# Row products of a patch-attention kernel, made once per feature row and kept

## The chip, the cores and the metric

The kernel runs on one core of a Trainium2 chip. The metric is the device time of one launch in microseconds (us), the median of several runs. In what follows TensorE is PE, VectorE is DVE, ScalarE is ACT, GpSimd is POOL, and SyncE (the engine that issues nearly all DMAs here) is SP.

## The reference

The input x has the shape (4, 64, 80, 80). Two identical layers of contextual attention run one after the other, each on 4 images, so there are eight units of work. One layer, cut to what matters:

```python
f = b[:, :, ::2, ::2]                                   # 64 x 40 x 40
w = 3x3 patches of f                                    # L = 1600 positions, 576 values each
wn = w / max(||w||, 1e-4)
yi = einsum('bpd,bld->blp', w, wn) * mm                 # 1600 x 1600 scores
yi = softmax(yi * 10, axis=1) * mm
patches = einsum('blp,bld->bpd', yi, 4x4 patches of b)  # pasted back with overlap
out = overlap_add(patches) / 4
```

The score of two positions is the sum, over the nine taps of a 3x3 window, of the products of 64 channels.

## The kernel before

**Tiles.** The 40 feature rows, padded to a pitch of 41, are laid out in 3 strips of 14 rows. A row tile holds the same row of the 3 strips, which is 3 x 41 = 123 positions (TW). There are 14 row tiles (TILES), worked on in 7 pairs (PAIRS), and 16 with the border. The scores of a unit, G, are a matrix of 14 x 14 blocks of 123 x 123; its columns are worked on in four chunks. S_CHUNKS (line 28) gives the chunks of the scores: 2, 4, 4 and 4 blocks. P_CHUNKS (line 27) gives those of the second part: 4, 4, 4 and 2. A "score pair" j (0 to 27) is one pair of row tiles t, t+1 (t = 2(j mod 7)) in one chunk k = j div 7. The matrix is symmetric before it is scaled, so blocks below the diagonal are not computed again: they are transposed on PE from blocks already in G.

**Three taps by three.** Call P(r, c) the product of feature row tile r with row tile c, summed over the three horizontal taps. The score block of row tile t and column s is P(t, s) + P(t+1, s+1) + P(t+2, s+2). Features are kept as a float16 high and low part, so that P(r, .) takes 5 matmuls (one_row, line 462): three of HL with LH, one of H1 with H1, one of HL with HL.

**A score pair with products (19 of the 28; nine more only transpose, and three of the 19 do both).** On PE even_tile (line 483) first makes the two rows that both tiles share, P(t+1)+P(t+2), as 9 matmuls in PSUM bank 2 (FREE), and then P(t) as 5 matmuls in bank 0. odd_tile (line 498) makes P(t+3) as 5 matmuls in bank 1; in ten pairs one column block can't use the shared rows and takes 14 matmuls of one block (TERMS, line 456 on), so such a pair has 33. ACT's copy_shared (line 656, activation in line 670) brings the shared rows from PSUM to the odd tile's place in G, one block further on (in the last chunk to S); copy_scores (line 672, activation in line 683) brings the transposed blocks and the lone blocks. DVE's score_pair (line 856) adds the shared rows to bank 0 for the even tile (tensor_tensor in line 881), takes the maximum of the scaled result (line 887, which also writes the scaled scores to S), adds and takes the maximum for the odd tile, and negates both maxima (line 892). Each maximum waits for the add in front of it on the same engine. ACT's score_sums (line 685, exp in line 697) then sums the exponentials of S.

**The other half of a slot.** The work is written out by hand in slots (body functions, s = 2 to 29), the same list on every engine, and skewed between units: while unit v's scores are made, unit u = v-1 goes through its second part. In each slot DVE runs, in this order, argument_pair (line 941) for the pair four slots on, add_shifted (line 952) for two slots on, after a shifted copy that SP issued as DMAs (SH<-G, line 326) has landed, sum_pair (line 974) for one slot on, and then score_pair. ACT runs the copies, with softmax_pair (line 708) between those of the even and of the odd tile, and then score_sums of the pair before. PE runs even_tile, two matmuls of paste_tile (line 521, float32, two records each), odd_tile and two more of paste_tile. Slots 16 and 21 hold two score pairs (score_list, line 48), slots 28 and 29 none. The features of the next unit but one are made in slots 5 and 6 on ACT (lines 612 to 624) and DVE (line 819), and laid out by SP in slots 10 to 12 (line 307: HL, H1, HV). SP stores results (line 314) in slots 8, 15, 22 and 29 and loads the next image (line 270) in slot 9. In slots 23, 24, 28 and 29 DVE and ACT work out the logarithms of the softmax sums (lines 906 to 931, 729, 734).

**Lead-in and tail.** Unit 0's scores have no second part beside them, and unit 7's second part has no scores beside it. Seven stretches hold both.

## Time and profile before

| | us |
|---|---|
| median of 3 runs | 1446.03 (1445.3 to 1454.68) |
| the profiled execution, its own time | 1450.82 |
| its span in the profile | 1449.0 |
| granted TensorE clock, mean | 0.986 of full |

The profile gives for each engine the time in which it was busy, the chain of work that ended last, and for each instruction group what ended the idle time before it. PE counts as busy until the modelled end of a matmul; matmuls overlap by about the time that one takes to drain, so the distance between two starts is what a matmul costs, and its own duration is more. The same is true on a smaller scale of DVE and ACT: an instruction that waits for nothing starts about 0.07 us before the one ahead has ended.

### The profile page before, as it was taken

The page shows a single profiled execution, that of the slowest core. Times are in us where ns is not written, and L with a number is a line of the kernel's source. Part 1 is how long each engine was busy: PE and PEld are TensorE (multiplying, and loading weights), DVE is VectorE, ACT ScalarE, POOL GpSimd, SP SyncE. Part 2 cuts the span into 40 slices and gives each one's busy share as a digit, 9 for nine tenths or more (in the row PEclk, how much of TensorE's full clock was granted, in tenths as well). Part 3 has the DMA queues.
Part 4 walks back from the last instruction along what each step waited for, and adds up shares of the span by engine and source line. Part 5 has one row for each costly group of instructions (what it writes and reads, how often), then busy time and mean ns, then how long its engine had stood idle before and what let it go on. Part 6 is the DMA issues. An engine that isn't in the chain of part 4 may idle for free.

```text
span 1449.0 us, 24232 instructions
## 1 busy us (share of the span) xinstructions
PE 1326.1 (92%) x7190; PEld 892.3 (62%) x7190; DVE 1190.6 (82%) x2827; ACT 856.0 (59%) x2233; POOL 46.8 (3%) x62
## 2 busy tenths in 40 slices
PE   4987999999999999999999899999999999998796
PEld 4756755667556765577556676566755676566333
DVE  4668889789887988888797898979988798978883
ACT  2667646666457664576455864567645765558331
POOL 1000000010000100001000010001000010000100
PEclk9997999999999999999999999999999999999999
DMA  5502482135822555135641357313582236313442
GB/s 90 88 1 84 108 172 74 45 112 119 164 63 60 129 111 148 49 85 129 128 121 34 92 127 161 89 45 99 122 169 65 63 105 136 99 36 86 133 137 55
DMA packets 180469, 142.53 MB, mean 98 GB/s; under 512 B 119858, under 2 KB 177266, under 8 KB 180338
## 3 DMA queue, kind: packets, MB, share of 16 engines
q1 hardware_dynamic: 180178, 140.50, 41.1%
q8 instruction: 57, 0.93, 0.3%
q10 hardware_dynamic: 160, 0.49, 0.2%
q14 instruction: 74, 0.61, 0.1%
HBM read 19.76 MB, written 13.11 MB: 23 GB/s over the span
## 4 chain that ended last, share of the span: by engine, by line
DVE 36%; PE 27%; issue 11%; ACT 9%; SPq 9%; DMA 6%; DVEq 1%; POOL 0%; ACTq 0%; POOLq 0%
PE psG L471 11%; PE psO L521 11%; DVE G L941 9%; DVE Z L974 7%; DVE G L881 5%; DVE S L887 5%; DVE G L952 5%; SPq L326 4%; DMA SH<-G 4%; ACT S L697 3%; PE psG L480 3%; ACT G L708 3%; SPq L270 2%; ACT G L683 2%; SPq L314 2%
## 5 line engine op out<-in xcount | busy, mean ns | idle before, releaser
L521 PE MATMUL psO<-Z,B 123*128 123x492 f32 (+2 forms) x1792 | 711.9, 526 | 41.5 <-DVE Z L974 29.6
L521 PEld LDWEIGHTS psO<-Z,B 123*128 123x128 f32 x1792 | 323.2, 193 | 240.2 <-issue 124.6
L471 PE MATMUL psG<-LH,HL 128*123 128x246 f16 (+2 forms) x2616 | 406.7, 285 | 13.6 <-DVE G L881 10.7
L471 PEld LDWEIGHTS psG<-LH,HL 128*123 128x123 f16 x2616 | 276.1, 137 | 136.7 <-issue 64.4
L708 ACT ACTIVATE G<-G,nb 123x492 f32<-123x492 f32 (+1 forms) x448 | 267.9, 642 | 137.4 <-DVE G L941 136.4
L887 DVE CUSTOM_DVE_ANT_0 S<-G,RB 123x492 f32<-123x492 f32 (+1 forms) x448 | 268.9, 606 | 86.7 <-DVE G L881 55.7
L697 ACT ACTIVATE S<-S,nm 123x480 f32<-123x480 f32 (+3 forms) x560 | 306.8, 554 | 1.8 <-DVE nm L892 1.6
L952 DVE TENSOR_TENSOR G<-G,SH 123x492 f32<-123x492 f32 (+1 forms) x448 | 246.9, 589 | 47.9 <-DMA SH<-G 47.8
L941 DVE SCALAR_TENSOR_TENSOR G<-G,RA,psB 123x492 f32<-123x492 f32 (+1 forms) x448 | 269.9, 645 | 0.0
L683 ACT ACTIVATE G<-psG 123x492 f32<-123x492 f32 (+3 forms) x256 | 119.6, 471 | 147.3 <-PE psG L480 69.1
L974 DVE TENSOR_TENSOR Z<-G 123x984 f32<-123x984 f32 (+2 forms) x192 | 196.8, 1025 | 0.0
L471 PE MATMUL psG<-H 128*123 128x123 f16 (+3 forms) x872 | 193.5, 283 | 0.0
L670 ACT ACTIVATE G<-psG 123x246 f32<-123x246 f32 (+1 forms) x136 | 64.1, 471 | 190.5 <-PE psG L471 190.1
L881 DVE TENSOR_TENSOR G<-G,psG 123x492 f32<-123x492 f32 (+2 forms) x272 | 133.8, 492 | 48.9 <-PE psG L471 28.2
L480 PEld LDWEIGHTS psG<-idn,G 123*123 123x123 f32 x672 | 95.6, 191 | 68.7 <-ACT G L683 22.7
L480 PE MATMUL psG<-idn,G 123*123 123x123 f32 x672 | 110.9, 285 | 23.9 <-ACT G L683 15.0
L471 PEld LDWEIGHTS psG<-H 128*123 128x123 f16 x872 | 102.3, 136 | 21.1 <-issue 0.4
L471 PE MATMUL psG<-HL 128*123 128x492 f16 (+2 forms) x392 | 111.5, 284 | 0.0
L697 ACT ACTIVATION_READ_ACCUMULATOR S<-S,nm 123x1 f32 x560 | 107.7, 192 | 0.0
L1082 POOL COPY G<-G 123x246 f32<-123x246 f32 x56 | 42.7, 771 | 1309.5 <-DVE mx L887 1175.7
L717 ACT ACTIVATE OSB<-psO 128x492 f32<-128x492 f32 (+2 forms) x64 | 31.4, 548 | 71.5 <-PE psO L521 71.3
L471 PE MATMUL psG<-HV 128*123 128x246 f16 (+2 forms) x240 | 67.5, 281 | 0.0
(79 smaller groups left out, 577.2 us busy)
## 6 DMA issues: line engine op xcount, KB each, us to landing
SH<-G SPq DMA_DIRECT2D x336, 214.8 KB
SH<-G SPq DMA_DIRECT2D x112, 89.2 KB
SH<-G SPq DMA_DIRECT2D x336, 19.2 KB
XP<-x SPq DMA_DIRECT2D x20, 280.0 KB, 5.5
XP<-mid SPq DMA_DIRECT2D x20, 280.0 KB, 5.3
HL<-LH SPq DMA_DIRECT2D x16, 246.5 KB, 4.3
mid<-OSB SPq DMA_DIRECT2D x48, 80.0 KB, 2.3
out<-OSB SPq DMA_DIRECT2D x48, 80.0 KB, 2.3
```

What stands on the lines that cost most here:

```text
L471: last = pe.matmul(psG[0:TW, bank, b0 * TW:b1 * TW], st[:, v % 2, p:p + TW], mv[:, v % 2, lo:lo + n], start=i == 0, stop=i == len(terms) - 1)
L480: last = pe.transpose(psG[0:TW, par, i * TW:(i + 1) * TW], G[:, c:c + TW], idn[0:TW, 0:TW])
L521: last = pe.matmul(psO[:, b, 0:n], B[:, o:o + 128], Z[:, 2 * (s % 2) + j, 0:n], start=t == 0, stop=t == TILES - 1)
L670: act.activation(to, psG[0:TW, FREE, stored * TW:w * TW], ACT.Copy).then_inc(p_copied, 1)
L683: act.activation(G[:, c:c + n], psG[0:TW, par, 0:n], ACT.Copy).then_inc(part if shared else read, 1)
L697: last = act.activation(y, y, ACT.Exp, bias=nm[:, k * TILES + t:k * TILES + t + 1], accum_out=sg[:, c:c + 1])
L708: act.activation(y, y, ACT.Exp, bias=nb[:, bass.ds(u * TILES + t, 1)]).then_inc(y_made, 1)
L881: dve.tensor_tensor((odd if par else even)[:, b0 * TW:n], rows[:, p0 * TW:p0 * TW + n - b0 * TW], psG[0:TW, par, b0 * TW:n], ALU.add).then ...
L887: dve.tensor_tensor_reduce(S[:, slot + par, 0:n], (odd if par else even)[:, 0:n], RB[:, s0 * TW:s0 * TW + n], 1.0, 0.0, ALU.mult, ALU.max, ...
L941: dve.scalar_tensor_tensor(out=g, in0=g, scalar=RA[:, bass.ds(u * TILES + t, 1)], in1=psB[0:TW, k % 2, 0:n], op0=ALU.mult, op1=ALU.subtrac ...
L952: dve.tensor_tensor(g, g, SH[:, o % SFREE, 0:n], ALU.add).then_inc(y1_made, 1)
L974: dve.tensor_tensor(Z[:, slot:slot + 2, 0:n], g[:, 2 * i:2 * i + 2, c0:c0 + n], g[:, 2 * i - 1:2 * i + 1, c0 - TW:c0 - TW + n], ALU.add).t ...
```

## The change

The kernel makes P(r, .) once for a chunk and keeps it. A score pair makes two rows, "row2" = P(t+2) and "row3" = P(t+3), 5 matmuls each; P(t) and P(t+1) are left from the pair before. At the start of a chunk's products "first" and "second" are made as well. The three PSUM banks are used in turn by a list of fills (FILLS, 67 a unit). ACT copies even rows to their own place in G and odd rows to a new tile ODD (copy_row), and for the chunk to the right it saves the fourth block of a row in KEPT and brings it back as the block in front of the next chunk's row. DVE does three additions (add_rows): two = ODD + row2, even = own + two, odd = two + row3. The odd tile's maximum and the negation of a pair are moved into the next pair's score_pair, between these additions; pairs 22 and 27 do them at once. The transposes of both tiles of pairs 9, 18 and 27 share a bank. HV and its two DMAs are gone. On ACT lse_log of slot 24 stands ahead of the second copy.

Counted over one unit, from the two lists: matmuls of products 515 (204 of one block, 140 of two, 5 of three, 166 of four) become 230 (30 of two, 30 of three, 170 of four); transposes stay 84. ACT's copies 51 become 104 (31 of three blocks, 42 of one, 18 of four, 13 of two; 18 of the single ones read KEPT). DVE's additions 38 become 58: (10 of two, 10 of one, 17 of four, 1 of three) become (20 of two, 11 of three, 26 of four, 1 of one). Maxima stay 56.

```diff
-def pair_blocks(j):
+def pair_of(j):
     k, t = j // PAIRS, 2 * (j % PAIRS)
     s0, w = S_CHUNKS[k]
-    if t < s0:
-        return w, w, w, 0
-    stored = t - s0 if t < s0 + w else 0
-    alone = stored + 1 if k in (0, NK - 1) or stored else 0
-    return w, stored, alone, w - stored
-SHARED = [j for j in range(SLOTS) if pair_blocks(j)[3]]
-EVEN_PARTS = [j for j in SHARED if pair_blocks(j)[1]]
-ODD_PARTS = [j for j in SHARED if pair_blocks(j)[2]]
+    return k, t, s0, s0 + w, s0 + w if t < s0 else t if t < s0 + w else s0
+def has_products(j):
+    k, t, s0, end, a = pair_of(j)
+    return a < end
+def is_start(j):
+    k, t, s0, end, a = pair_of(j)
+    return j == 0 or (k > 0 and t == s0 - 2)
+def shared_from(j):
+    k, t, s0, end, a = pair_of(j)
+    return a - 1 if k == 0 or t > s0 and a > s0 else a
+def fills_of(j):
+    k, t, s0, end, a = pair_of(j)
+    if not has_products(j):
+        return ["even", "odd"] + (["first", "second"] if is_start(j) else [])
+    return (["first", "second"] if is_start(j) else []) + ["row2", "row3"] + (["both"] if a > s0 else [])
+PRODUCTS = [j for j in range(SLOTS) if has_products(j)]
+FILLS = [(j, kind) for j in range(SLOTS) for kind in fills_of(j)]
+COPIED = [(j, kind) for j, kind in FILLS if kind in ("row2", "row3") and pair_of(j)[1] < TILES - 2]
+def row_of(j, kind):
+    k, t, s0, end, a = pair_of(j)
+    base = 0 if j == 0 else s0
+    return {"first": base, "second": base + 1, "row2": t + 2, "row3": t + 3}[kind]
+def takes_kept(j, kind):
+    k, r = j // PAIRS, row_of(j, kind)
+    return k > 0 and (kind in ("first", "second") or r >= 4 * k + 2)
+def keeps(j, kind):
+    k, r = j // PAIRS, row_of(j, kind)
+    return k < NK - 1 and (j, kind) in COPIED and r >= 4 * k + 2
+TAKEN = [(j, kind) for j, kind in FILLS if ((j, kind) in COPIED or kind in ("first", "second")) and takes_kept(j, kind)]
...
-            TERMS = [(HL, LH, dy, dx) for dy in range(3) for dx in range(3)]
-            TERMS += [(H1, H1, dy, 0) for dy in range(3)]
-            TERMS += [(HV, HV, 0, 2), (HL, HL, 2, 2)]
-            SHARED_ROWS = [(HL, LH, dy, dx) for dy in (1, 2) for dx in range(3)]
-            SHARED_ROWS += [(H1, H1, 1, 0), (H1, H1, 2, 0), (HV, HV, 1, 2)]
-            def one_row(dy):
-                return [(HL, LH, dy, dx) for dx in range(3)] + [(H1, H1, dy, 0), (HL, HL, dy, 2)]
...
+            ROW = [(HL, LH, dx) for dx in range(3)] + [(H1, H1, 0), (HL, HL, 2)]
+            def products(v, j, kind):
+                k, t, s0, end, a = pair_of(j)
+                c0, r = 4 * k, row_of(j, kind)
+                b0, b1 = 0, 4
+                if kind in ("first", "second"):
+                    b1 = 2 if kind == "first" else 3
+                elif t == TILES - 2:
+                    b0 = (shared_from(j) if kind == "row2" else a) + 2 - c0
+                n, bank = fill(v, j, kind)
+                if n >= BANKS:
+                    pe.wait_ge(released[bank], n // BANKS)
+                for i, (st, mv, dx) in enumerate(ROW):
+                    lo, p = (c0 + b0) * TW + dx, r * TW + dx
+                    last = pe.matmul(psG[0:TW, bank, b0 * TW:b1 * TW], st[:, v % 2, p:p + TW],
+                                     mv[:, v % 2, lo:lo + (b1 - b0) * TW], start=i == 0, stop=i == len(ROW) - 1)
+                last.then_inc(filled, 1)
+            def transposes(v, j, kind):
+                k, t, s0, end, a = pair_of(j)
+                n, bank = fill(v, j, kind)
+                pe.wait_ge(*done(v, (k - 1) * PAIRS + (s0 + 2) // 2 if t < s0 else j - 1, "row3"))
+                pe.sem_inc(pe_gate, 1)
+                pe.wait_ge(released[bank], n // BANKS)
+                o = 0
+                for tile in {"even": (t,), "odd": (t + 1,), "both": (t, t + 1)}[kind]:
+                    for s in range(s0, min(a, end)):
+                        c = s * GLEN + tile * TW
+                        last = pe.transpose(psG[0:TW, bank, o:o + TW], G[:, c:c + TW], idn[0:TW, 0:TW])
+                        o += TW
+                last.then_inc(filled, 1)
+            def first_half(v, j):
+                if not has_products(j):
+                    transposes(v, j, "even")
+                    return
+                if is_start(j):
+                    products(v, j, "first")
+                    products(v, j, "second")
+                products(v, j, "row2")
...
+            def copy_row(u, v, j, kind):
+                k, r = j // PAIRS, row_of(j, kind)
+                n, bank = fill(v, j, kind)
+                even, start = r % 2 == 0, kind in ("first", "second")
+                if even:
+                    columns_free(u, k, r)
+                    blocks = 3 if keeps(j, kind) else 2
+                    c = r * GLEN + 4 * k * TW
+                    to = G[:, c:c + blocks * TW]
+                    before = G[:, c - TW:c]
+                else:
+                    blocks = 3
+                    slot = 0 if j == 0 and start else (j + 1) % 2
+                    to = ODD[:, slot, TW:4 * TW]
+                    before = ODD[:, slot, 0:TW]
+                    reader = last_products(v, j)
+                    if reader[0] >= 0:
+                        act.wait_ge(*done(*reader, "row2"))
+                        act.sem_inc(act_gate, 1)
+                if takes_kept(j, kind):
+                    act.wait_ge(row_copied, copied(v, (k - 1) * PAIRS + (r - 2) // 2, "row3" if r % 2 else "row2"))
+                    act.activation(before, KEPT[:, r - 2, :], ACT.Copy).then_inc(kept_taken, 1)
+                act.wait_ge(filled, n + 1)
+                last = act.activation(to, psG[0:TW, bank, 0:blocks * TW], ACT.Copy)
+                if keeps(j, kind):
+                    if takes_kept(j, kind):
+                        act.wait_ge(kept_taken, v * len(TAKEN) + TAKEN.index((j, kind)) + 1)
+                    last = act.activation(KEPT[:, r - 2, :], psG[0:TW, bank, 3 * TW:4 * TW], ACT.Copy)
+                if start:
+                    last.then_inc(released[bank], 1)
+                else:
+                    last.then_inc(row_copied, 1)
...
                     if s % PAIRS == 0 and v is not None:
                         score_sums(v, score_list(s - 1)[0] - 1)
                     for n, j in enumerate(pairs):
-                        if pair_blocks(j)[3]:
-                            copy_shared(u, v, j)
-                        copy_scores(u, v, j, 0)
+                        copy_first(u, v, j)
                         if at and n == 0 and s != 24:
                             softmax_pair(at)
-                        copy_scores(u, v, j, 1)
+                        if s == 24:
+                            lse_log(v, False)
+                        copy_second(u, v, j)
                         if s == 23:
                             lse_exp(v, False)
-                        if s == 24:
-                            lse_log(v, False)
                         if j and (s + 1) % PAIRS:
                             score_sums(v, j - 1)
...
-            def score_pair(v, j):
+            def add_rows(u, v, j):
+                k, t, s0, end, a = pair_of(j)
+                qa, c0 = shared_from(j), 4 * k
+                n = (end - qa) * TW
+                slot = 2 * (j % 2) + 1
+                cols = lambda tile, s, e: G[:, tile * GLEN + s * TW:tile * GLEN + e * TW]
+                two = cols(t + 1, qa + 1, end + 1) if k < NK - 1 else S[:, slot, (qa - s0) * TW:(end - s0) * TW]
+                rows = lambda kind, c, e: psG[0:TW, fill(v, j, kind)[1], (c - c0) * TW:(e - c0) * TW]
+                if k == NK - 1:
+                    dve.wait_ge(s_read, v * NB + 2 * j + 2)
+                    dve.sem_inc(dve_gate, 1)
+                elif u is not None:
+                    if k == 0:
+                        dve.wait_ge(wrap_made, u * PAIRS + min(t // 2 + 2, PAIRS))
+                        dve.sem_inc(dve_gate, 1)
+                    dve.wait_ge(z_made, u * SLOTS + k * PAIRS + min(t // 2 + 2, PAIRS) + 1)
+                    dve.sem_inc(dve_gate, 1)
+                if (j, "row2") in COPIED:
+                    dve.wait_ge(row_copied, copied(v, j, "row2"))
+                else:
+                    dve.wait_ge(row_copied, copied(v, j - 1, "row3"))
+                    dve.sem_inc(dve_gate, 1)
+                    dve.wait_ge(filled, fill(v, j, "row2")[0] + 1)
+                o = (qa - c0 + 2) * TW
+                dve.tensor_tensor(two, ODD[:, j % 2, o:o + n], rows("row2", qa + 2, end + 2),
+                                  ALU.add).then_inc(done(v, j, "row2")[0], 1)
+                yield
+                dve.wait_ge(*done(v, j, "row2"))
+                own = cols(t, a, end)
+                dve.tensor_tensor(own, own, two[:, (a - qa) * TW:n], ALU.add).then_inc(even_added, 1)
+                yield
+                dve.wait_ge(even_added, v * len(PRODUCTS) + count(PRODUCTS, j))
+                dve.sem_inc(dve_gate, 1)
+                if (j, "row3") in COPIED:
+                    dve.wait_ge(row_copied, copied(v, j, "row3"))
+                else:
+                    dve.wait_ge(filled, fill(v, j, "row3")[0] + 1)
+                b = a
+                if k == NK - 1 and qa == a:
+                    first = cols(t + 1, a, a + 1)
+                    dve.tensor_tensor(first, first, rows("row3", a + 2, a + 3), ALU.add).then_inc(odd_begun, 1)
+                    b = a + 1
+                odd = cols(t + 1, b, end)
+                with_two = odd if k < NK - 1 else two[:, (b - 1 - qa) * TW:(end - 1 - qa) * TW]
+                dve.tensor_tensor(odd, with_two, rows("row3", b + 2, end + 2),
+                                  ALU.add).then_inc(done(v, j, "row3")[0], 1)
...
+            def score_pair(u, v, j):
+                adds = add_rows(u, v, j) if has_products(j) else iter(())
+                next(adds, None)
+                if j - 1 not in (-1, 22):
+                    maxima(v, j - 1, 1)
+                next(adds, None)
+                if j - 1 not in (-1, 22):
+                    negate(v, j - 1)
+                next(adds, None)
+                maxima(v, j, 0)
+                if j in (22, SLOTS - 1):
+                    maxima(v, j, 1)
+                    negate(v, j)
```

## Rows read from the trace of the kernel before

**Rows 1.** The page, part 1: busy us (share of the span) xinstructions
```profile
PE 1326.1 (92%) x7190; PEld 892.3 (62%) x7190; DVE 1190.6 (82%) x2827; ACT 856.0 (59%) x2233; POOL 46.8 (3%) x62
```

**Rows 2.** Windows, busy (xcount), of one full unit by chunk of the scores
```profile
839.90:875.10 35.20, 34.08 (x260) 25.70 (x259) 31.88 (x77) 23.00 (x58) 1.84 (x2) 1.00 0.51 123
875.10:923.80 48.70, 48.37 (x205) 28.11 (x205) 42.32 (x88) 24.80 (x57) 0.00 (x0) 1.00 0.69 148
923.80:961.00 37.20, 35.21 (x160) 21.19 (x158) 30.65 (x78) 21.57 (x55) 0.00 (x0) 1.00 0.19 52
961.00:997.50 36.50, 33.49 (x207) 26.12 (x208) 29.74 (x80) 29.69 (x90) 0.00 (x0) 1.00 0.31 85
```

**Rows 3.** The chain that ended last, in order of time: start, length, what
```profile
919.63 1.18 DVE Z L974
...
930.95 1.66 PE psO L521 x4
```

**Rows 4.** Timeline of DVE, one slot with a four-block pair (pair 11)
```profile
910.58 1.36 DVE L941 SCALAR_TENSOR_TENSOR G<-G,RA,psB 123x492 f32<-123x492 f32 x2
...
914.11 0.66 DVE L881 TENSOR_TENSOR G<-G,psG 123x492 f32<-123x492 f32 x1
914.96 0.67 DVE L887 CUSTOM_DVE_ANT_0 S<-G,RB 123x492 f32<-123x492 f32 x1 [0.19 <-DVE G L881]
...
915.55 0.67 DVE L881 TENSOR_TENSOR G<-G,psG 123x492 f32<-123x492 f32 x1
...
917.20 0.72 DVE L941 SCALAR_TENSOR_TENSOR G<-G,RA,psB 123x492 f32<-123x492 f32 x1
```

**Rows 5.** Groups by form, DVE's additions of fewer blocks
```profile
L881 DVE TENSOR_TENSOR G<-G,psG 123x246 f32<-123x246 f32 x72 | 29.0, 403 | 10.5 <-PE psG L471 6.4 <-ACT G L670 3.0 <-ACT G L683 1.1
L881 DVE TENSOR_TENSOR G<-G,psG 123x123 f32<-123x123 f32 x72 | 20.1, 279 | 15.6 <-ACT G L683 14.8
L881 DVE TENSOR_TENSOR G<-S,psG 123x369 f32<-123x369 f32 x8 | 4.3, 535 | 0.6 <-ACT G L683 0.5 <-issue 0.2
```

**Rows 6.** Timeline of PE: products of four blocks, and of one
```profile
705.79 1.41 PE L471 MATMUL psG<-LH,HL 128*123 128x492 f16 x6
...
716.78 0.68 PE L471 MATMUL psG<-LH,HL 128*123 128x123 f16 x9
```

**Rows 7.** Timeline of ACT (exps of one pair, next copy); groups of copies
```profile
909.12 0.69 ACT L697 ACTIVATE S<-S,nm 123x480 f32<-123x480 f32 x1
...
910.47 0.57 ACT L670 ACTIVATE G<-psG 123x492 f32<-123x492 f32 x1
...
L683 ACT ACTIVATE G<-psG 123x123 f32<-123x123 f32 x64 | 17.0, 266 | 33.6 <-PE psG L471 33.5
...
L683 ACT ACTIVATE G<-psG 123x369 f32<-123x369 f32 x24 | 11.5, 478 | 26.8 <-PE psG L471 26.7
```

**Rows 8.** Waits of DVE over the whole span: us in total, times, longest
```profile
DVE S L887 <- DVE G L881: 55.7, 295, 0.5
DVE G L952 <- DMA SH<-G: 47.8, 30, 5.5
```

**Rows 9.** Waits of DVE in 936 to 961 us (pairs 17 to 20)
```profile
DVE G L881 <- PE psG L471: 2.1, 3, 1.2
DVE G L881 <- ACT G L683: 1.7, 1, 1.7
```

**Rows 10.** Waits of DVE in 961 to 997.5 us (chunk 3)
```profile
DVE S L887 <- ACT G L683: 2.1, 4, 0.9
DVE sg L916 <- ACT S L697: 1.0, 1, 1.0
...
DVE G L881 <- ACT S L670: 0.9, 1, 0.9
DVE tot L929 <- ACT lns L734: 0.8, 1, 0.8
```

**Rows 11.** Windows of unit 0 without a second part: chunks 1 and 3
```profile
52.20:78.70 26.50, 25.28 (x153) 17.81 (x152) 18.04 (x52) 14.69 (x41) 0.00 (x0) 1.00 0.61 101
...
103.00:133.60 30.60, 23.55 (x149) 19.14 (x148) 21.65 (x62) 26.84 (x85) 0.00 (x0) 0.83 0.23 67
```

More of the change, by code:

```diff
@@ L109, in contextual_attention @@
         S = sb("S", [TW, 2 * FREE, 4 * TW], F32)
+        KEPT = sb("KEPT", [TW, TILES - 2, TW], F32)
+        ODD = sb("ODD", [TW, 2, 4 * TW], F32)
         OSB = sb("OSB", [128, 4 * STRIPS, 2 * PITCH], F32)
@@ L859, in score_pair @@
                 n = w * TW
[L860 removed]
+                if i == 0 and par == 0 and k != 1:
                     dve.wait_ge(r_rows, v * 4 + max(k + 1, 2))
                     dve.sem_inc(dve_gate, 1)
[L863 to L867 removed]
```

224 lines of the change are left out of this document (101 added, 123 removed).

## The prediction

> **What bounds the kernel now.** I read the page's busy shares first: PE 92%, DVE 82%, ACT 59% [rows 1]. Taken alone they say that PE is the bound and that fewer matmuls are worth what they cost. The chain of waits says otherwise: inside one unit it runs on DVE in some stretches and on PE in others. A piece on DVE's sum for pair 12 and one on PE's paste matmuls for pair 15 show the two kinds [rows 3]. So I read one unit by chunk [rows 2]. In chunks 0 and 1 (839.9 to 923.8) PE is busy 34.1 of 35.2 us and 48.4 of 48.7, but DVE is packed too: a slot of chunk 1 lasts 6.62 us (917.20 - 910.58) and DVE's instructions stand end to end in it, but for two gaps of 0.19 us in which a maximum waits for DVE's own addition [rows 4]. In chunk 2 (923.8 to 961.0) DVE has 30.65 us of work in 37.2; in 936 to 961 it waits 2.1 us for PE's products and 1.7 for ACT's copy of blocks that PE transposed late [rows 9]. In chunk 3 it has 29.74 in 36.5 and waits mostly for ACT [rows 10]. PE's spare time is worth something only where DVE waits for PE, directly or through ACT.
>
> **PE.** Six four-block matmuls span 1.41 us with a last one of about 0.37, so one costs (1.41 - 0.37)/5 = 0.21 us; nine of one block span 0.68 with a last one of 0.22, so 0.057 each [rows 6]. A two-block one lies between, 0.10. Before: 204 x 0.057 + 140 x 0.10 + 5 x 0.155 + 166 x 0.21 = 61 us a unit. After: 170 x 0.21 + 30 x 0.155 + 30 x 0.10 = 43. So 18 us of PE go in each unit, 146 in eight; a four-block pair goes from 19 x 0.21 = 4.0 us to 2.1. If PE were the bound everywhere that would be 10% of the time.
>
> **DVE.** A four-block pair now costs 917.20 - 914.11 = 3.09 us: an addition to the start of its maximum 0.85 (work and the wait for itself), the maximum 0.59, both twice, and the negation 0.20 [rows 4]. An addition that nothing waits for costs 0.59, since 0.66 overlaps the next by 0.07. In the new order the row sum (0.59) is followed by the old pair's odd maximum (0.59), then the even addition, behind which the third one must wait for it (0.85, with the negation inside that wait), then the third addition (0.59) and the even maximum (0.59): 3.23. The additional pass thus costs 0.14, not 0.66, because the moved maximum and negation fill the self-waits, of which the whole trace has 55.7 us [rows 8]. That an addition of SBUF with SBUF costs what one with PSUM costs is bounded by add_shifted and L881, both 0.66 for four blocks. For a two-block pair the three additions are of three, two and two blocks, 0.535, 0.403, 0.403 us, for 0.403 and 0.279 [rows 5]: by the same sum +0.13. I charge 7 x 0.13 + 4 x 0.14 = 1.5 us a unit in chunk 0 and the last four pairs of chunk 1. Pairs 8 and 9 are free: there DVE waits for the shift DMAs behind the image loads in SP's queue (most of the 47.8 us [rows 8]), and whatever DVE loses is taken from that wait.
>
> **ACT.** 51 copies become 104. By durations of 0.48 for three blocks and 0.27 for one [rows 7], and 0.58 for four, it is 24 us a unit before and 41 after; the 18 copies out of KEPT read SBUF, which the trace shows for no plain copy this small: I take PSUM's 0.27, between 0.2 and 0.4, which moves the sum by 3 us at most, off the path where ACT has room. ACT would go from 856 us to about 990 of 1449: hidden in sum, not in every place. Also, the negation comes half a pair later, behind it the exps of that pair take 910.47 - 909.12 = 1.35 us [rows 7], and behind them, in ACT's order, stand the next pair's first copy and all that it serves. In an ordinary slot DVE has 3.54 us of second-part work (914.11 - 910.58 [rows 4]) before it wants that copy, which covers it. I find four places with less cover:
> - Slot 6, where the feature conversion (about 2.2 us) is behind the exps: row copies late, DVE waits +0.5.
> - Slot 16 with pairs 14 and 15: the exps of 13 are now in front of 15's copy, +0.3.
> - Slot 23: the log sum needs the exps of 22 and loses the cover of a moved maximum: +0.4.
> - Slots 25 and 26: four extra copies (1.2 us), and the third addition's one-block piece in pair 26: +0.5 in all, with that pair's and 27's additions.
>
> A rule of the Trainium skill speaks against this part: "VectorE: DVE Perf Modes", section "The TRN2 errata", says that ScalarE and VectorE pay a fixed cost per instruction, so that many small tiles cost more than one large one. This trace agrees: one block takes 0.27 us and three blocks 0.48, so about 0.16 is fixed. It is in the durations above and adds nothing to the sum.
>
> **What comes back.** In chunk 2 DVE's idle time is 37.2 - 30.65 = 6.5 us [rows 2], of which 8 x 0.19 = 1.5 is waits for itself. Of the other 5 I take back 4.1, where PE and the late bank made it wait [rows 9], pay 0.6 for the additions of pairs 17 to 20 and 0.3 for slot 16: -3.2. In chunk 3 the waits for transposed blocks (2.1) and for the logarithm (0.8, now ahead of a copy) mostly go; those for exps (1.0) and for the copy behind DVE's own sum (0.9) stay [rows 10]: -2.5 + 0.4 + 0.5 = -1.6. A full unit: +1.5 + 0.5 - 3.2 - 1.6 = -2.8 us, and seven of them -20. Late next is DVE itself, with ACT some tenths behind.
>
> Unit 0 has no second part: there PE is busy 25.3 of the 26.5 us of chunk 1 [rows 11], 4.0 us a pair, and the next bound is DVE's 3.23, ACT's exps and row copies (up to 1.35 + 1.6 = 3.0) just below. Five pairs there and four of chunk 2 win about 0.65 each, -6; chunk 0 loses its gain to ACT's copies, chunk 3 wins 1. So -7. The tail has no scores and doesn't move. The two HV transfers of slot 12 are gone from SP, behind the image loads for which DVE waited; I cost them at nothing, since pairs 10 to 13 wait for no DMA (pair 11 is shown [rows 4]).
>
> Sum: -27. Against the profiled execution 1450.8 - 27 = 1424; the median of the runs shown is 4.8 lower, 1446.0 - 27 = 1419.
>
> **Rivals.**
> - *A: as summed, 1419* (1402 to 1432 by its own terms). For: PE-bound stretches are clear in the chain; DVE's self-waits are there to be filled.
> - *B: DVE fully packed.* PE a pair and a half ahead of DVE also removes the waits for ACT. A full unit's idle time that isn't DVE waiting for itself is about 9.3 us in chunks 2 and 3; all of it gone less 2.6 of additions is -6.7, seven times -47, lead-in -12: 1387. Against: ACT's exps stay in the chain.
> - *C: only chunk 2 wins.* ACT sets chunk 3's pace (29.7 busy of 36.5 before the new copies [rows 2]) and returns nothing there: 1.5 + 0.5 - 3.2 + 0.5 = -0.7 a unit, lead-in -4: 1446 - 9 = 1437.
> - *D: slower, by ACT.* The place is ACT's queue between a negation and the next row copy. If the two together (exps 1.35, features, softmax 1.3, copies 1.6) reach past DVE's 3.54 us of cover, each pair of chunks 0 to 2 waits. It decides from about 0.3 us past the cover in 19 pairs: +5.7 a unit on top of C's -0.7, +5 x 7 = +35, lead-in 0: 1481. With only slots 6, 16, 23 and 25 to 27 hit, 1.2 us each, it is 1462. For: in slot 6 and 23 I find the cover gone. Against: in chunk 1 ACT is busy 24.8 of 48.7 [rows 2].
>
> **Chances.** A 0.47, B 0.11, C 0.24, D 0.10, E 0.08. Faster by over 1% (below 1431.6) is B, most of A and a part of C: 0.60. Within 1%, about what a measurement of this kernel can tell from no change, 0.25. Slower by over 1% (above 1460.5): D and half of E, 0.15. The range takes in B's and C's sides and the smaller half of D: 1390 to 1458.
>
> **What the profile after would show.** PE busy about 1180 to 1200 us with 2280 fewer matmuls; DVE's busy time up by about 100 us to 1290, with the wait of a maximum for an addition nearly gone; ACT near 990. The slot of chunk 1 goes from 6.62 to about 6.76 us, the slots of pairs 18 and 19 from 6.5 and 7.1 to about 5 and 5.6. The SH<-G wait of pair 9 stays at 4 to 5 us. I am wrong if DVE's additions wait for row copies on ACT in ordinary slots (D), if the granted clock in the middle is below 0.97 (E), if the slots of pairs 17 to 20 don't shrink (C or worse), or if DVE's other waits fall below about 8 us a unit (B).

## The result and the profile after

The changed kernel takes 1454.87 us (median of 20 runs, 1451.88 to 1459.49), the kernel before 1448.65 beside it (20 runs, 1444.08 to 1454.68). The ratio is 1.0043, with a 95% interval of 1.0033 to 1.0054: 0.4% slower, where 27 us less was forecast. The profiled execution took 1452.66 us, with a span of 1450.8 and a mean granted clock of 0.941.

The page of the kernel after, parts 1, 2 (the clock in 40 slices), 4 and two groups of part 5. They answer to [rows 1] and, for the exps, to [rows 7].

```profile
PE 1233.3 (85%) x4910; PEld 767.0 (53%) x4910; DVE 1254.1 (86%) x2987; ACT 953.4 (66%) x2657; POOL 46.8 (3%) x62
...
PEclk9988999999999999999999999999999999999899
...
DVE 40%; ACT 14%; issue 13%; PE 13%; SPq 12%; DMA 6%; DVEq 0%; POOL 0%; ACTq 0%; POOLq 0%
...
L800 ACT ACTIVATE S<-S,nm 123x480 f32<-123x480 f32 (+3 forms) x560 | 308.8, 556 | 208.2 <-DVE nm L1034 207.4
```

PE has 2280 matmuls fewer, as the change says, and it is no longer the busiest engine. A 9 of the clock row stands for 90% and more, so the fall of the clock is read from the mean: 0.941, for 0.986 before. The last row is the one to stop at: before its exps ACT now stands idle 207 us, waiting for DVE's negation. ACT executes in order, so all that stands behind those exps, the next pair's row copies first, waits with them. Whether that matters depends on what DVE does in that time.

Windows of one full unit after, cut where sum_pair starts in slots 2, 9, 16, 21 and 28 (columns: stretch, its length, busy us (xcount) of PE, PEld, DVE, ACT, POOL, granted clock, DMA share, GB/s):

```profile
841.13:882.32 41.19, 37.70 (x150) 22.99 (x149) 39.24 (x93) 27.83 (x72) 2.77 (x3) 0.92 0.51 118
882.32:932.39 50.07, 44.84 (x166) 24.70 (x165) 44.76 (x94) 31.14 (x84) 0.00 (x0) 1.00 0.66 135
932.39:961.01 28.62, 26.17 (x100) 14.86 (x100) 26.73 (x72) 20.74 (x62) 0.00 (x0) 1.00 0.19 53
961.01:1004.24 43.23, 34.92 (x176) 26.66 (x174) 36.87 (x97) 34.59 (x108) 0.73 (x2) 0.92 0.27 74
```

The same four stretches of the same unit before, cut at the same slots ([rows 2] cut it elsewhere):

```profile
837.07:877.61 40.54, 39.41 (x292) 29.61 (x290) 36.81 (x90) 25.33 (x62) 2.77 (x3) 1.00 0.50 119
877.61:926.25 48.64, 47.72 (x201) 27.46 (x199) 42.26 (x89) 24.80 (x57) 0.00 (x0) 1.00 0.70 149
926.25:958.29 32.04, 30.81 (x142) 18.80 (x143) 25.67 (x69) 17.32 (x47) 0.00 (x0) 1.00 0.17 49
958.29:1000.01 41.72, 37.41 (x221) 28.09 (x219) 34.77 (x90) 34.69 (x107) 0.73 (x2) 1.00 0.28 76
```

Length after less length before: +0.65, +1.43, -3.42, +1.51. The gain of slots 16 to 20 is there, and the other three give it back. One unit scatters, so I also took the distance from the sum_pair of a slot to that of the next slot on DVE, as a mean over units 1 to 6, in us. The slots left out change by 0.2 or less each:

| slots | before | after | |
|---|---|---|---|
| 2 | 5.28 | 6.18 | +0.90 |
| 4 | 5.88 | 5.33 | -0.55 |
| 6 | 7.41 | 7.73 | +0.32 |
| 13 to 15, each | 6.63 | 6.71 | +0.07 |
| 16 | 6.57 | 6.56 | 0 |
| 17 to 20, sum | 25.01 | 22.39 | -2.62 |
| 21 | 8.16 | 7.23 | -0.93 |
| 22 | 3.75 | 6.32 | +2.57 |
| 24 | 6.68 | 5.69 | -0.99 |
| 25 and 26, sum | 12.95 | 12.23 | -0.72 |
| 27 | 5.79 | 6.65 | +0.86 |
| a unit, 28 slots | | | about -0.7 |

By the start of each unit's first sum_pair, the lead-in (unit 0) ends at 137.8 us for 130.2, +7.6; from there to the start of the last unit the kernel wins 6.7; the tail costs 0.9. Sum +1.8, as the spans have it (1450.8 - 1449.0).

The waits over the whole span after, those that answer to [rows 8] and those that are new or have grown:

```profile
ACT S L800 <- DVE nm L1034: 207.4, 134, 6.3
...
DVE G L1111 <- DMA SH<-G: 38.8, 24, 4.7
...
PE psG L534 <- DVE G L983: 34.5, 17, 5.4
...
PE psG L549 <- DVE G L1004: 31.8, 19, 4.7
...
DVE S L1028 <- ACT G L727: 28.3, 38, 1.6
```

And two of them as they were before:

```profile
DVE S L887 <- ACT G L683: 26.6, 44, 1.4
...
PE psG L480 <- DVE G L881: 8.1, 18, 1.6
```

Before's 55.7 us in which a maximum waited for DVE's own addition [rows 8] have no counterpart: that part of the change did what was forecast. The wait for the shift DMAs fell from 47.8 to 38.8, where DVE's additional work went at no cost. PE's waits for DVE's additions have grown: its products wait 34.5 us for the first addition (L983) and its transposes 31.8 us for the third (L1004), where before the two kinds waited 10.7 and 8.1 us. The maxima's wait for transposed blocks (L1028 for L727), most of which the forecast took back in chunk 3, is no smaller than before, 28.3 us for 26.6. Both come back below. DVE's timeline of a slot of chunk 1 with a four-block pair, which answers to [rows 4]:

```profile
912.27 0.66 DVE L1129 TENSOR_TENSOR Z<-G,SHJ 123x492 f32<-123x492 f32 x1
912.85 0.67 DVE L1130 TENSOR_TENSOR Z<-G 123x492 f32<-123x492 f32 x1
913.43 0.66 DVE L983 TENSOR_TENSOR G<-ODD,psG 123x492 f32<-123x492 f32 x1
914.00 0.67 DVE L1028 CUSTOM_DVE_ANT_0 S<-G,RB 123x492 f32<-123x492 f32 x1
...
914.60 0.67 DVE L988 TENSOR_TENSOR G<-G 123x492 f32<-123x492 f32 x1
915.18 0.17 DVE L1034 TENSOR_SCALAR nm<-mx 123x2 f32<-123x2 f32 x1
915.41 0.67 DVE L1004 TENSOR_TENSOR G<-G,psG 123x492 f32<-123x492 f32 x1
916.00 0.66 DVE L1028 CUSTOM_DVE_ANT_0 S<-G,RB 123x492 f32<-123x492 f32 x1
...
916.59 1.36 DVE L1100 SCALAR_TENSOR_TENSOR G<-G,RA,psB 123x492 f32<-123x492 f32 x2
```

A pair takes 916.59 - 913.43 = 3.16 us for 3.09, with three additions for two: the moved maximum and the negation fill the places in which DVE waited for itself.

A part of what the lead-in lost stands ahead of all pairs. The first maximum starts 3.35 us later; PE first makes four rows, two of them four blocks wide:

```profile
31.41 0.42 DVE L887 CUSTOM_DVE_ANT_0 S<-G,RB 123x246 f32<-123x246 f32 x1 [0.19 <-DVE G L881]
...
34.76 0.41 DVE L1028 CUSTOM_DVE_ANT_0 S<-G,RB 123x246 f32<-123x246 f32 x1
```

(The first line is the kernel before, the second the kernel after.) Where more of the lead-in went is in the chain of the kernel after (start, length, what):

```profile
67.62 1.47 ACT S L800 x4
69.08 0.20 ACT G L753
...
69.54 0.26 ACT KEPT L759
...
70.42 0.67 DVE S L1028
71.09 0.58 DVE G L988
71.67 0.09 DVE nm L1034
71.78 1.47 ACT S L800 x4
```

It is a closed loop: the exps of a pair, behind them in ACT's order the next pair's row copies, behind those DVE's first addition and maximum, the even addition, the negation, and then exps again. One turn takes 71.78 - 67.62 = 4.16 us, and the next set of exps starts another 4.53 later, at 76.31. Before, the pair there took 3.95.

And what slot 22 gives back begins in slot 21. The timeline of the kernel after, PE and DVE from the end of pair 20 into pairs 21 and 22, which only transpose:

```profile
960.04 1.27 PE L586 MATMUL psO<-Z,B 123*128 123x328 f32 x4
...
963.75 0.67 DVE L1004 TENSOR_TENSOR G<-G,psG 123x492 f32<-123x492 f32 x1
...
964.56 1.16 PE L549 MATMUL psG<-idn,G 123*123 123x123 f32 x4 [3.25 <-DVE G L1004]
...
965.51 2.30 PE L586 MATMUL psO<-Z,B 123*128 123x328 f32 x4
...
966.52 0.67 DVE L1028 CUSTOM_DVE_ANT_0 S<-G,RB 123x492 f32<-123x492 f32 x1 [0.72 <-ACT G L727]
...
971.34 0.67 DVE L1028 CUSTOM_DVE_ANT_0 S<-G,RB 123x492 f32<-123x492 f32 x1 [1.35 <-ACT G L727]
```

PE stands 3.25 us before the transposes of the next pair, for DVE's third addition, and then runs at the lower clock: the same four transposes take 1.16 us there and 0.59 at 968.53, the same four paste matmuls 2.30 for 1.27. DVE then waits for ACT's copies of the transposed blocks.

### The profile page after: what moved, and what is told of

Read it like the earlier page. It is cut to its first block, busy times and chain, and to the rows that moved or that the text cites. A ratio compares the mean times of both kernels' runs of the same rounds, so it can differ in the third digit from the quotient of the medians.

```text
span 1450.8 us, 20009 instructions
## 1 busy us (share of the span) xinstructions
PE 1233.3 (85%) x4910; PEld 767.0 (53%) x4910; DVE 1254.1 (86%) x2987; ACT 953.4 (66%) x2657; POOL 46.8 (3%) x62
## 4 chain that ended last, share of the span: by engine, by line
DVE 40%; ACT 14%; issue 13%; PE 13%; SPq 12%; DMA 6%; DVEq 0%; POOL 0%; ACTq 0%; POOLq 0%
DVE G L1100 8%; DVE S L1028 8%; DVE Z L1133 8%; PE psO L586 7%; SPq L389 6%; ACT S L800 6%; DVE G L1111 5%; PE psG L534 4%; DVE G L988 3%; DVE G L983 3%; DMA SH<-G 3%; SPq L333 3%; ACT G L811 3%; DMA SHJ<-G 2%; SPq L377 2%
## 5 line engine op out<-in xcount | busy, mean ns | idle before, releaser
L586 PE MATMUL psO<-Z,B 123*128 123x492 f32 (+2 forms) x1792 | 748.2, 549 | 83.3 <-DVE Z L1133 47.9
L534 PE MATMUL psG<-LH,HL 128*123 128x492 f16 (+2 forms) x1104 | 278.9, 362 | 49.8 <-DVE G L983 34.5
L1028 DVE CUSTOM_DVE_ANT_0 S<-G,RB 123x492 f32<-123x492 f32 (+1 forms) x448 | 267.7, 602 | 30.1 <-ACT G L727 28.3
L1111 DVE TENSOR_TENSOR G<-G,SH 123x492 f32<-123x492 f32 (+1 forms) x448 | 247.3, 591 | 38.9 <-DMA SH<-G 38.8
L534 PEld LDWEIGHTS psG<-LH,HL 128*123 128x123 f16 x1104 | 145.0, 139 | 173.9 <-issue 70.9
L549 PE MATMUL psG<-idn,G 123*123 123x123 f32 x672 | 112.8, 297 | 41.2 <-DVE G L1004 31.8
L534 PE MATMUL psG<-H 128*123 128x492 f16 (+2 forms) x368 | 131.5, 357 | 0.0
L727 ACT ACTIVATE G<-psG 123x492 f32<-123x492 f32 x192 | 96.5, 524 | 40.0 <-PE psG L549 31.4
L755 ACT ACTIVATE ODD<-psG 123x369 f32<-123x369 f32 x152 | 72.0, 474 | 65.4 <-PE psG L534 64.2
L983 DVE TENSOR_TENSOR G<-ODD,psG 123x369 f32<-123x369 f32 (+1 forms) x136 | 80.9, 595 | 29.4 <-ACT KEPT L759 21.4
L755 ACT ACTIVATE G<-psG 123x369 f32<-123x369 f32 (+1 forms) x152 | 65.8, 433 | 51.4 <-PE psG L534 50.2
L1004 DVE TENSOR_TENSOR G<-G,psG 123x246 f32<-123x246 f32 (+1 forms) x136 | 72.4, 532 | 22.8 <-ACT KEPT L759 9.9
L988 DVE TENSOR_TENSOR G<-G 123x246 f32<-123x246 f32 (+1 forms) x136 | 72.4, 533 | 0.3
```

Of the source, the lines that this page charges most:

```text
L534: last = pe.matmul(psG[0:TW, bank, b0 * TW:b1 * TW], st[:, v % 2, p:p + TW], mv[:, v % 2, lo:lo + (b1 - b0) * TW], start=i == 0, stop=i == ...
L549: last = pe.transpose(psG[0:TW, bank, o:o + TW], G[:, c:c + TW], idn[0:TW, 0:TW])
L586: last = pe.matmul(psO[:, b, 0:n], B[:, o:o + 128], Z[:, 2 * (s % 2) + j, 0:n], start=t == 0, stop=t == TILES - 1)
L755: last = act.activation(to, psG[0:TW, bank, 0:blocks * TW], ACT.Copy)
L983: dve.tensor_tensor(two, ODD[:, j % 2, o:o + n], rows("row2", qa + 2, end + 2), ALU.add).then_inc(done(v, j, "row2")[0], 1)
L988: dve.tensor_tensor(own, own, two[:, (a - qa) * TW:n], ALU.add).then_inc(even_added, 1)
```

## The experiments

All ratios are against the kernel before in the same batch (its medians were 1447.6 to 1448.9 us), with their 95% interval. Three theories stood against each other at first: a wait of PE that is wider than it need be (slots 21 and 22), the order of ACT's exps and row copies (the lead-in), and PE's clock.

**A narrower wait.** The transposes read tiles of earlier chunks, and the wait asks for the pair just before. Here it asks for the addition that makes the last of the rows that they read, in the chunk that these lie in.

```diff
-  pe.wait_ge(*done(v, (k - 1) * PAIRS + (s0 + 2) // 2 if t < s0 else j - 1, "row3"))
+  left = next(c for c in range(NK) if t < sum(S_CHUNKS[c]))
+  pe.wait_ge(*done(v, left * PAIRS + (s0 + 2) // 2 if t < s0 else j - 1, "row3"))
```

> The changed kernel, but a pair that only transposes waits for the last addition of the chunk that its blocks lie in, no longer for the newest one (pairs 21 to 23, 14 and 15 are freed). Gate theory: in slot 21 PE stands idle 3.3 us behind the third addition of pair 20, then works at half clock, and DVE loses 2.6 us in slot 22; that goes in seven units, 1454.9 to about 1438 (ratio to before 0.993), and the half-clock stretches after slot 21 go too. If the exps on ACT set slots 21 and 22 instead, the copies come no earlier: 1452 to 1456. If PE's clock as such is the cause, half-clock time stays near 175 us and so does the time.

1435.71 us, 0.9907 (0.9874 to 0.9940): 19 us under the changed kernel, as expected. The timeline of the same place in this kernel:

```profile
951.77 0.67 DVE L1005 TENSOR_TENSOR G<-G,psG 123x492 f32<-123x492 f32 x1
...
952.49 0.69 PE L550 MATMUL psG<-idn,G 123*123 123x123 f32 x4 [0.73 <-DVE G L1005]
...
953.01 1.27 PE L587 MATMUL psO<-Z,B 123*128 123x328 f32 x4
```

The wait is 0.73 for 3.25 us, the paste matmuls behind it keep their 1.27, and slot 22 goes from 6.32 to 4.25 us, slot 21 from 7.23 to 6.78.

**The exps behind the next pair's first copy**, in slots 2 to 20: ACT keeps a pair's exps back until copy_first of the next pair is issued; flush runs score_sums for all that is held.

```diff
+  held = []
...
   copy_first(u, v, j)
+  flush()
...
-  score_sums(v, j - 1)
+  held.append(j - 1)
+  if s >= 21:
+      flush()
```

> The changed kernel, but on ACT the exps of a pair stand behind the next pair's first copy (slots 2 to 20). Loop theory: without a second part beside them the pairs turn in a loop, negation, exps 1.5 us, row copy, first addition, maximum, second addition, negation, 4.2 to 4.5 us a pair; taking the exps out of it brings unit 0 back to about 3.3 us a pair: 6 to 10 us less in the first 140 us, 1446 to 1449 in all (ratio 0.999), full units unchanged to 1 us. If PE's half clock sets unit 0, or DVE's work does, the lead-in stays at 137.8 us and the time at 1453 to 1456.

1435.02 us, 0.9906 (0.9875 to 0.9937), 20 us under the changed kernel, more than twice what was expected. The lead-in ends at 124.8 for 137.8 us, 13 where 6 to 10 were expected, and the full units win 0.9 us each: slot 16 goes from 6.56 to 5.98. The chain of this kernel in the lead-in:

```profile
59.80 1.34 ACT S L800 x4
61.15 0.19 ACT ODD L753
61.34 0.37 ACT ODD L755
61.71 0.16 ACT KEPT L759
61.88 0.53 ACT G L727 x2
...
62.82 0.31 ACT KEPT L759
63.13 1.35 ACT S L800 x4
...
66.28 1.35 ACT S L800 x4
```

The loop through DVE is gone: the chain stays on ACT and turns in 3.33 and 3.15 us.

**The negation in its own pair.** The same loop can be cut at the other end: second maximum and negation return to the pair that they belong to, and DVE waits for itself again.

```diff
   next(adds, None)
-  if j - 1 not in (-1, 22):
-      maxima(v, j - 1, 1)
   next(adds, None)
-  if j - 1 not in (-1, 22):
-      negate(v, j - 1)
   next(adds, None)
   maxima(v, j, 0)
-  if j in (22, SLOTS - 1):
-      maxima(v, j, 1)
-      negate(v, j)
+  maxima(v, j, 1)
+  negate(v, j)
```

> The changed kernel, but a pair's second maximum and its negation stand in their own pair again, so the additions wait for each other and nothing fills the gaps. DVE theory: 0.5 us more in each of the pairs where DVE is the bound (about 12 a unit, slots 2 to 17), +6 a unit, but the exps are half a pair earlier: slot 22, slot 23 and the lead-in win back 3 a unit and 7 once. Sum 1455 + 21 - 7 = 1468. If the late negation is the main loss, the time falls below 1450.

1458.04 us, 1.0079 (1.0052 to 1.0106), 3 us over the changed kernel where 13 were expected. The lead-in shortens too, to 129.5 us, but each slot of chunk 1 is 0.32 us longer, and slot 21 is 9.88 us long. As the kernel stood, the moved maximum was worth only these 3 us.

**PE kept busy.** Two further matmuls ahead of each row, into the same bank; the row's own first one overwrites them.

```diff
+  for st, mv, dx in ROW[:2]:
+      pe.matmul(psG[0:TW, bank, b0 * TW:b1 * TW], ..., start=True, stop=True)
```

> The changed kernel with two matmuls more in front of each row (their result is overwritten), 92 more a unit, 18 us of PE a unit at full clock, as much as the change took away. If the granted clock is what cost the gain (half clock for 175 us in place of 41), this keeps PE busy, half-clock time falls below 80 us and the time falls below 1450. If PE's work in slots 21 and 22 and in the lead-in is on the path, the time rises by 5 to 15 us (1460 to 1470). If PE plays no part at all, 1453 to 1457.

1472.11 us (1463.9 to 1482.8), 1.0146 (1.0100 to 1.0192), at a granted clock of 0.974 for 0.941. The clock came back and the time went up by 17 us. The filler is work too, so this run doesn't price the clock by itself; it shows that buying the clock back with work doesn't pay. That the low clock isn't the main cost is shown by the two edits above: each won 20 us, at 0.951 and 0.942.

**Narrow wait and late exps together**, and then, over it, the second maximum of pair 23 in its own pair (slot 24).

> The changed kernel with both edits of the first two runs: the transposes wait only for what they read, and the exps stand behind the next first copy. They took away 20 us each, one in slots 21 and 22 of the full units, the other in the lead-in and slots 16 to 20. If they are two separate causes, the gains add: 1455 - 39 = 1416 to 1422 (ratio to before 0.977 to 0.982). If both remove one and the same delay of PE, the second adds little: 1430.

> The same, and pair 23's second maximum and negation in their own pair. In slot 23 the log sum waits 1.9 us for the exps of pair 22; the 0.8 us of the maximum and negation would lie in that wait, and slot 24 would be 0.8 shorter: 7 x 0.7 = 5 us below e5_both. If ACT's exps set slots 23 and 24 in any case, no difference (within 1 us).

The first took 1414.86 us, 0.9770 (0.9734 to 0.9806): the two gains add (19 + 20 under 1454.9 is 1415.9). The second took 1409.09, 0.9733 (0.9711 to 0.9756), with slot 24 at 5.26 for 5.69 us. The two intervals overlap, so only the shorter slot, some 3 us in seven, is clear of the scatter.

**The second copy of slot 2 ahead of its softmax**, over the version just above, for the +0.9 of that slot:

> e6_both_own23, and in slot 2 ACT makes its second copy ahead of the softmax of the second part. There the four row copies of a unit's first pair keep DVE's third addition waiting 1.1 us; it then waits 0 to 0.3: 0.8 a unit, 6 us: 1401 to 1405 (ratio 0.969). If the later softmax makes the shift DMAs late instead, the gain returns as a wait for SH in slots 4 and 5 and the time stays at 1409.

1407.63 us, 0.9730 (0.9704 to 0.9757): no different from the version without it, and slot 2 is 6.33 for 6.24 us. Another miss; what lengthens slot 2 stays open.

**What fewer matmuls are worth alone.** The kernel before with ten products a pair for 19 and everything else as it was. It leaves out terms of the products, so its scores are incomplete.

```diff
+  TERMS, SHARED_ROWS = TERMS[:7], SHARED_ROWS[:2]
...
-  return [(HL, LH, dy, dx) for dx in range(3)] + [(H1, H1, dy, 0), (HL, HL, dy, 2)]
+  return [(HL, LH, dy, dx) for dx in range(3)] + [(H1, H1, dy, 0)]
```

> The kernel before with fewer matmuls and nothing else changed: the shared rows keep 2 of 9, a single row 4 of 5, a lone block 7 of 14, so a pair has 10 for 19 (17 for 33), and the scores are left incomplete. It shows what PE's 18 to 20 us a unit are worth by themselves. Prediction's step: only chunk 2, a part of chunk 3 and the lead-in return something, 4 to 6 us a unit and 10 to 20 once: 1395 to 1415. If PE is the bound, seven times 18: 1300 to 1330. If its spare time is worth nothing even alone: 1440 or more.

1426.62 us, 0.9859 (0.9831 to 0.9888), at a clock of 0.942: 21 us, and less than I expected. The edit takes more from PE than the change does, since the blocks stay narrower: the trace has 80 fewer matmuls of four blocks a unit, 80 of two and 87 of one, by the prediction's prices 30 us a unit and not the 18 to 20 of the expectation. Still the slots of chunk 1 (11 to 15) are what they were to 0.01 us, which is the plainest proof that DVE bounds them; in chunk 0 only slot 4 is over 0.1 us shorter (5.88 to 5.68). The waits over the whole span, PE's two kinds and DVE's own:

```profile
PE psG L472 <- DVE G L882: 83.9, 74, 5.1
...
PE psG L481 <- DVE G L882: 70.2, 35, 3.3
...
DVE S L888 <- DVE G L882: 57.2, 303, 0.5
```

PE now waits 154 us for DVE's additions. Its clock fell as far as in the changed kernel, and the kernel was faster all the same.

**The narrower wait in the kernel before.**

> The kernel before with only the narrower wait: the transposes of a pair wait for the odd addition of the chunk that they read, not for the newest one. The same wide wait stood here, but the addition that it names came half a pair sooner. If the half-pair shift made it costly, the kernel before gains little: slot 21 (8.2 us, 1.3 of it a wait for transposed blocks) gets 0 to 0.7 shorter, 0 to 5 us in all (ratio 0.997 to 1.0). If the wait was as costly here, 15 to 20 us go (0.988).

1431.50 us, 0.9898 (0.9870 to 0.9926). A miss: I had taken the wait for harmless there. It cost before 16.5 us, spread over slots 16 (6.57 to 5.94), 18, 19 and 21 (8.16 to 7.55), and so is for the most part no cost of the change, which pays 19 for it and gathers it in slots 21 and 22.

**The kernel before with both edits**, and with the narrow wait and fewer matmuls (its scores again incomplete):

> The kernel before with the narrower wait (1431.5 us, e9) and with the exps behind the next pair's first copy as in e5_both. If the loop over negation, exps, row copy and addition is the changed kernel's own, since only there the negation comes half a pair late and each row is copied, nothing is gained here: 1429 to 1434 (ratio 0.988 to 0.991), and the changed kernel loses about 20 us by it. If ACT's order costs both, this falls to 1412 to 1420.

> e7_before_fewer (10 matmuls a pair for 19, scores left incomplete, 21 us below the kernel before) with the narrower wait. Slots 16 and 21 had become longer there (7.4 and 8.8 us), so part of PE's saving stood behind the wide wait. If so the two add up to more than their sum (21 + 16): 1400 to 1411. If both only empty the same stretches, 1415 to 1425.

1423.08 us (1422.96 to 1431.55), 0.9849 (0.9815 to 0.9883), and 1399.20, 0.9681 (0.9647 to 0.9715). The first lies between its two forecasts. Late exps are worth some 8 us to the kernel before (1431.5 - 1423.1, four runs each from two batches, with intervals that meet) and 20 to the changed one, so about half of those 20 or more come with the change. And with the wait mended, fewer matmuls alone are worth 32 us; the two edits together win 49, more than their sum of 37.

**More copies on ACT**: the changed kernel with 24 further copies of 104 columns a unit.

```diff
+  act.activation(JUNK[:, r - 2, :], psG[0:TW, bank, 3 * TW:3 * TW + 104], ACT.Copy)
```

> The changed kernel with one more copy of 104 columns on ACT wherever a row's last block is kept (24 a unit, about 0.25 us each, 6 us of ACT a unit). If ACT's copies as such are what ate the gain, this costs nearly as much again: 24 x 0.25 x 7 = 40 us, 1485 or more. If ACT has room in the full units and stands in a loop only in unit 0, the cost is below 8 us: 0.25 to 0.5 a pair in the lead-in (+4) and a little in slot 2 and 6: 1457 to 1463.

1459.01 us, 1.0075 (1.0050 to 1.0101), 4 us more for 192 copies. In most slots of the full units ACT has room for copies; where it has not is slot 2 (6.18 to 7.03) and slot 6 (7.73 to 7.97). In the loop of the lead-in a pair gets 0.15 us longer (pair 9, from even maximum to even maximum, 4.57 for 4.42), but the lead-in as a whole ends at 137.2 for 137.8 us; the 4 us expected there didn't come.

**The moved maximum and the filler again, in the mended order.** The two edits of above, over the 1414.86 and the 1409.09 version.

> e5_both, but each pair's second maximum and negation in its own pair again. With the two losses of the late negation mended, only its gain is left to lose: 0.32 us in each of some 15 pairs a unit where DVE is the bound, 5 a unit, 35 in seven, and 5 in the lead-in: 1450 to 1458 (ratio 1.003 to 1.008). If the late negation is worth nothing once the exps stand late, it is at 1415 to 1425.

> e6_both_own23 with two matmuls more in front of each row, 18 us of PE a unit, so that PE has as much to do as in the kernel before. It shows what the change's smaller PE work is worth in the mended order. By the slots, PE is close to the bound in slots 19 to 22 and the lead-in alone: +15 to +30 us, 1424 to 1440. If PE's clock matters more than its work, the time does not rise (1405 to 1412).

1436.83 us, 0.9932 (0.9908 to 0.9956), +22; and 1447.54, 1.0008 (0.9989 to 1.0027), +38 at a clock of 0.973. The first cost less than I expected, the second more. Slots 5 (5.42 to 7.44) and 19 (5.86 to 7.42) take most of the second. The same edits cost 3 and 17 us in the kernel as it was changed: with the two orders mended, the moved maximum and PE's saved time are both worth more.

## Why the prediction was wrong, step by step

**What bounds the kernel: right.** DVE in chunks 0 and 1, PE in chunk 2. Fewer matmuls alone change next to nothing in the former.

**PE: right.** (Eight times its 18 us are 144, not 146.) Ten four-block products take 2.1 us: five of them start at 944.06 in the timeline after and the next instruction at 945.10. Busy time ended at 1233 and not at 1180 to 1200, since PE runs at the lower clock more often.

**DVE: right in kind, too dear.** (The terms of its new order add up to 3.21, not 3.23.) An additional pass costs 0.07 us, not 0.14 for a four-block pair: the third addition starts 0.81 us behind the even one, not 0.85, and the row sum takes 0.57, not 0.59. Chunks 0 and 1 got 1.2 us longer a unit for 1.5 + 0.5, though not evenly: slots 2 and 6 gained 1.22, slot 4 lost 0.55. So the total is partly luck. The additions' own durations grew by 13.1 us a unit, 105 in eight, as forecast; busy time is 1254 and not 1290, since instructions that follow one another overlap. Pairs 8 and 9 (slots 10 and 11) were nearly free, 0.20 and 0.07 us.

**ACT: the sum right.** The copies take 24 us a unit before and 41 after, as summed; busy time is 953 us and not 990, again since neighbours overlap. The copy out of KEPT takes 0.30 us, where I took 0.27 between 0.2 and 0.4; the 0.27 and 0.48 from which the prediction took a fixed part were copies out of PSUM. Of the four places with little cover slot 6 cost 0.3 (forecast 0.5) and slot 16 nothing in sum. Slot 23 stayed as it was, 4.88 us. Slots 25 and 26 got 0.72 us shorter. Slot 27, whose pair I had in the last group, cost 0.86, and slot 2, which I hadn't, 0.90.

**"What comes back", chunk 2, -3.2: right.** Slots 16 to 20 won 2.6 in the mean and 3.4 in the unit shown. The two slots that I named, those of pairs 18 and 19, are 19 and 20. From the first argument of a slot to that of the next, as the prediction cut them, they went from 6.54 to 5.15 us ("about 5") and from 8.12 to 7.19 in the mean. The second was said to go from 7.1 to 5.6: the 7.1 is what one unit of the six shows, and the slot won 0.9 us, not 1.5.

**"Chunk 3, -1.6": failed.** The slots of chunk 3 (21 to 27) came to +0.8 in sum. I took back the waits for transposed blocks as if a PE with less to do had to be earlier. But PE's transposes wait for DVE's last addition of the pair before, and that addition is now the third, further back. PE's saved time turned into waiting in front of that semaphore. Reading who releases the transposes, and not only who waits for them, would have shown it: with the narrow wait slots 21 and 22 lose 2.5 us in each unit (7.23 + 6.32 to 6.78 + 4.25), or 18 in seven, of the 19 measured. And chunk 3 as a whole is then 1.8 us shorter than before, close to the -1.6: the step that failed is the wait, not the rest of the sum.

**"Unit 0, -7": failed, with +7.6 measured.** These 14.6 us are the larger of the two misses; the full units missed by 13. The sum there took PE's 4.0 us as the price of a pair before, set DVE's 3.23 and ACT's 3.0 side by side, and took the larger as the price after. They don't run side by side. I had seen in the text that ACT's exps stand in front of the next copies and named DVE's 3.54 us of second-part work as the cover. Unit 0 has no second part and so no cover; there, exps, copies, first addition, maximum, even addition and negation follow each other in a loop of 4.2 to 4.5 us, more than the 3.95 of before. This is rival D's mechanism in the one place where I had put its price at zero ("lead-in 0"). With the exps behind the copy, pairs 9 to 12 take 3.2 us, the nine pairs that were to win 6 us (9 to 13, 17 to 20) win 6.3 where they had won 1.1, and the lead-in ends 5.4 us earlier than before, close to the -7.

The loop isn't all of it. The first maximum is 3.35 us late (with the exps behind the copy it still starts at 34.08 us), and three pairs (7, 16 and 25) take, from even maximum to even maximum, 6.57, 6.87 and 8.13 us for 3.44, 4.72 and 6.76. They run partly at the lower clock. In pair 7 the price can be read. PE's 16 small matmuls of the next features, before and after:

```profile
50.64 1.83 PE L395 MATMUL psM<-halves,SQ 128*123 128x2 f32 x16
...
52.78 3.27 PE L458 MATMUL psM<-halves,SQ 128*123 128x2 f32 x16
```

With the eight transposes behind them they take 4.9 us (52.78 to 57.70) for 2.6 (50.64 to 53.27), at a granted clock of 0.50 for 1.00, after PE had waited 2.39 us for a first addition (L983). That is 2.3 of the pair's 3.1 us. For pairs 16 and 25, and for the late start, the cause wasn't separated.

**A full unit, -2.8 seven times: -1.0 in its place** (6.7 us in all). The failing term is chunk 3, and behind it slots 2 and 27.

**Rivals.** C had the right size in a full unit (-0.7) and the wrong lead-in. E's sign was there, 0.95 in the middle of the kernel, and E was right in pair 7 and behind PE's long waits, but not as the main cause: both edits won 20 us at nearly the same low clock, putting the clock back by more matmuls made the kernel slower, and fewer matmuls in the kernel before made it faster at 0.942. (PE was busy 95% and more in three of the four chunks on which E rests; in chunk 3 it was 92%.) By the Trainium skill, "TensorE: Matmul & The Clock Gate", Part 1, a less busy PE loses its higher clock, and the trace agrees (the mean went from 0.986 to 0.941); but it lost it in the places where it waits for others.

**What the change is worth.** With both edits in both kernels, 1414.9 against 1423.1 us: 8 us by the medians and 11 by the ratios (0.9770 and 0.9849, each with some 5 us to either side), and a few more with pair 23's maximum in its place. In the order that it came in, the loop ate that. The best version (1407.6 to 1409.1 us) is 2.7% faster than the kernel before and 3.2% faster than the changed one. The split of the last microseconds between slots 2 and 27, the late start and the low clock stays open.

## What to carry to other kernels

When an edit takes work from one engine, follow the semaphores that this engine waits for, not only its queue: what it saves turns into waiting where a wait names a later producer than the data need. When a step is delayed (here a negation by half a pair), write down the whole ring of engines through which it comes back to itself and add it up in each stage, with and without the other stage's work as cover; a stage without cover runs at the ring's length, not at the busiest engine's. And before a kernel is judged slower, try the order of one engine's instructions: here one narrowed wait and one moved group of instructions were worth 40 us of 1455, where the change itself is worth about 10.

## What the runs showed of the hardware

VectorE's wait for its own last result can be filled wholly: 295 waits of 0.19 us are gone with one independent instruction between, and in a four-block pair an additional pass of 0.66 us cost 0.07.

TensorE came back from an idle stretch of 3.25 us at the lower of its two clocks (four transposes in 1.16 us for 0.59, granted clock 0.56 from 964.5 to 968.0), and the four paste matmuls behind took 2.30 us for 1.27. Over the whole kernel the mean clock didn't tell which version was faster: 1426.6 us at 0.942, 1472.1 at 0.974, where the second also had more work.

ScalarE's copy of 123 columns from SBUF took 0.30 us (955.06 in the timeline after) and from PSUM 0.27.
